# Joining the taps above and below in an HetConv stage: 64x32 tiles over a stacked copy of the image

## What is computed

```
x = x + _L1_conv_ref(_gn(x), L1_conv_W, L1_conv_b, 4)

_gn: 32 groups of 4 channels, mean and variance over (4, 32, 32), (v - m) / sqrt(s + 1e-5)
_L1_conv_ref:
    is3x3 = (i - n) % 4 == 0              # input channel i, output channel n
    Wm = W * where(is3x3, ones(3,3), centre only)
    y = conv 3x3, padding 1, of x with Wm
    return y + sum(b, axis=1)
```

## Time and profile before

| what | value |
|---|---|
| runs, median of three | 695.71 us (691.93 to 696.08) |
| profiled execution, device time | 695.91 us |
| its span in the trace | 694.0 us |
| mean granted TensorE clock | 0.957 |
| PE busy over the span | 586.4 us (84%) |
| DVE, ACT, POOL busy | 490.5, 489.1, 250.3 us |
| last stage, first to last `conv_done` | 461.18 to 685.71 us of the span |

### The profile page before, as it was taken

How to read it: one execution, slowest core, us unless ns; L and a number is a source line. 1 busy time by engine, 2 the same in 40 slices (tenths; PEclk the granted TensorE clock), 3 DMA queues, 4 the chain that set the end, 5 groups by cost and what they waited for, 6 DMA issues and landing times.

```text
span 694.0 us, 23636 instructions
## 1 busy us (share of the span) xinstructions
PE 586.4 (84%) x9897; PEld 416.7 (60%) x9897; DVE 490.5 (71%) x1172; ACT 489.1 (70%) x870; POOL 250.3 (36%) x253
## 2 busy tenths in 40 slices
PE   1899799899999999999999999386677876768882
PEld 1344344588888888888888887154454544444451
DVE  5788973599999999999999999864345454433220
ACT  2688688899999999999999998543335443333520
POOL 2478667445555555555555555300000000000000
PEclk9899899999999999999999999699999999998997
DMA  9989900022344444432224440013222333222343
GB/s 226 251 236 259 204 4 0 1 37 42 46 62 62 62 61 62 62 58 43 43 43 62 60 63 1 0 35 95 65 64 70 81 92 75 64 66 64 72 97 84
DMA packets 85002, 53.38 MB, mean 77 GB/s; under 512 B 71200, under 2 KB 72480, under 8 KB 84896
## 3 DMA queue, kind: packets, MB, share of 16 engines
q1 hardware_dynamic: 84224, 51.07, 36.9%
q10 hardware_dynamic: 672, 0.79, 0.5%
HBM read 35.07 MB, written 16.78 MB: 75 GB/s over the span
## 4 chain that ended last, share of the span: by engine, by line
PE 73%; issue 11%; DVE 8%; ACT 3%; SPq 1%; POOL 1%; DMA 1%; DVEq 0%; ACTq 0%; POOLq 0%
PE ps L1102 16%; PE ps L1181 15%; PE ps L1080 11%; PE ps L1107 8%; PE ps L1159 7%; PE ps L1084 5%; PE ps L1025 4%; PE ps L1026 3%; PE ps L1169 2%; DVE bn L416 2%; SPq L286 1%; DMA img<-in_x_dram 1%; POOL lo L755 1%; ACT xn L824 1%; ACT hi L834 1%
## 5 line engine op out<-in xcount | busy, mean ns | idle before, releaser
L1102 PE MATMUL ps<-z_hi,wg_hi 128*128 128x352 f32 (+13 forms) x384 | 134.2, 351 | 3.3 <-ACT z_hi L882 3.3
L774 POOL TENSOR_TENSOR fc<-gate,cell 128x352 f32<-128x352 f32 (+16 forms) x96 | 83.8, 873 | 144.1 <-ACT gate L898 144.1
L1102 PE MATMUL ps<-z_hi,wg_lo 128*128 128x352 f32 (+13 forms) x384 | 122.2, 319 | 0.0
L952 ACT ACTIVATE img<-ps,finish 128x512 f32<-128x512 f32 x32 | 23.1, 773 | 137.9 <-PE ps L1181 137.9
L1107 PE MATMUL ps<-z_lo,wg_hi 128*128 128x352 f32 (+13 forms) x384 | 107.5, 321 | 0.0
L898 ACT ACTIVATE gate<-ps,gate_bias 128x352 f32<-128x352 f32 (+16 forms) x192 | 104.1, 542 | 1.3 <-PE ps L1107 1.3
L683 DVE TENSOR_SCALAR img<-ps,finish 128x512 f32<-128x512 f32 x32 | 24.9, 805 | 110.8 <-PE ps L1181 110.8
L898 ACT ACTIVATE ps<-ps,gate_bias 128x352 f32<-128x352 f32 (+16 forms) x192 | 99.5, 518 | 0.0
L1181 PE MATMUL ps<-pad,wall_hi 32*32 32x512 f16 x3072 | 79.7, 408 | 15.9 <-issue 15.9
L784 POOL TENSOR_TENSOR img<-hT,xr 128x352 f32<-128x352 f32 (+1 forms) x96 | 88.6, 923 | 1.7 <-DVE hT L639 1.7
L755 POOL TENSOR_TENSOR lo<-xn,hi 128x1024 f16<-128x1024 f32 x32 | 68.0, 2131 | 32.4 <-ACT hi L834 31.8
(11 more groups left out here) (131 smaller groups left out, 1263.7 us busy)
## 6 DMA issues: line engine op xcount, KB each, us to landing
xr<-in_x_dram SPq DMA_DIRECT2D x64, 256.0 KB, 5.6
out_dram<-img SPq DMA_DIRECT2D x64, 256.0 KB
img<-in_x_dram SPq DMA_DIRECT2D x126, 128.0 KB, 3.6
raw_c<-in_L_conv_W_dram SPq DMA_DIRECT2D x4, 144.0 KB, 2.9
img<-in_x_dram ACTq DMA_DIRECT2D x2, 128.0 KB, 3.2
raw_g<-in_L_conv_w_ih_dram SPq DMA_DIRECT2D x1, 256.0 KB, 8.9
raw_i<-in_L_conv_w_i2s_dram ACTq DMA_DIRECT2D x1, 192.0 KB, 5.4
raw_s<-in_L_conv_w_s2s_dram ACTq DMA_DIRECT2D x1, 192.0 KB, 5.7
```

Of the source, the lines that this page charges most:

```text
L774: pool.tensor_tensor(fc[it % 2][:, 0:c1 - c0], gate[it % 2][0][:, 0:c1 - c0], cell[:, c0:c1], ALU.mult).then_inc(fc_done, 1)
L1102: pe.matmul(gbank(it, m)[:, 0:n], w[:, GATE_ORDER[m], :], z_hi[it % 2][:, 0:n], start=(w is wg_hi), stop=False)
```

## The change

The six taps above (d = 0) and below (d = 2) an image row no longer run as 32x32 tiles in groups 1 to 15. For every image from the third on, GpSimd copies the padded slot twice (`stack`, k = 0 and 1), and SyncE then overwrites, by four transfers from `pad`, the 32 partitions of the neighbouring class in each copy with the same class's image shifted by two rows. A 64-partition half of the stack so holds one class twice, as it stands and two rows further down, and one 64x32 tile multiplies it with the weights of both taps (`wk_hi`, `wk_lo`, placed once by sixteen small transfers). That is 3 terms x 3 columns x 2 x 8 = 144 matmuls; the side taps (`SIDES`) stay, 3 x 2 x 16 = 96. Group 0 keeps all of its 384.

The statistics are regrouped: of the upper image halves of eight images that VectorE measured during LSTM items 88 to 95, four are now measured during items 60, 68, 76 and 84, the other four images whole after the LSTM, between the first `lo` calls. The second chunk's `sum_means`, `sum_vars`, square root and `chain_rstd` come later in group 0.

```diff
+UPPER_AT = (60, 68, 76, 84)
+SIDES = [(1, 0), (1, 2)]
+TWO_ROWS = 2 * (W + 1)
...
+            stack = [[sb(f"stack{i}{k}", [P, PADT], F16, s2) for k in range(2)] for i in range(SLOTS)]
...
+            def place_blocks():
+                sp.wait_ge(split_done, 3 + 3)
+                for t, src in ((wk_hi, wall_hi), (wk_lo, wall_lo)):
+                    for q in range(Q):
...
+                        sp.dma_start(t[r, q % 2], src[r, 0, :, r]).then_inc(blocks_in, 16)
+                        sp.dma_start(t[other, q % 2], src[r, 2, :, r]).then_inc(blocks_in, 16)
+            def stack_below(b):
+                sp.wait_ge(stacked, 2 * (b - PAIR + 1))
+                for q in range(Q):
+                    sp.dma_start(stack[b % SLOTS][q % 2][32 * (q ^ 1):32 * (q ^ 1) + 32, 0:PADT - TWO_ROWS],
+                                 pad[b % SLOTS][32 * q:32 * q + 32, TWO_ROWS:PADT]).then_inc(below_in[b % SLOTS], 16)
...
+            stack_below(PAIR)
+            stack_below(PAIR + 1)
             for g in range(GROUPS):
                 sp.wait_ge(out_act, len(ACT_CLASSES) * (g + 1))
                 sp.wait_ge(out_dve, len(DVE_CLASSES) * (g + 1))
                 store_group(sp, g, range(Q))
+                for b in range(PAIR * (g + 2), min(PAIR * (g + 3), B)):
+                    stack_below(b)
...
-                if ITEMS - HELD <= it < ITEMS:
-                    if it == ITEMS - HELD:
-                        v.wait_ge(row_done, ROW_AHEAD + NB * H // 2)
-                    upper_stats(it - (ITEMS - HELD))
+                if it in UPPER_AT:
+                    v.wait_ge(row_done, ROW_AHEAD + NB * H // 2)
+                    upper_stats(UPPER_AT.index(it))
...
+                if g == 0:
+                    chain_var(FIRST_CHUNKS + 1)
+                    chain_rstd(FIRST_CHUNKS + 1, 1)
...
+            for b in range(PAIR, B):
+                pool.wait_ge(lo_done, b + 1)
+                if b >= PAIR + SLOTS:
+                    pool.wait_ge(conv_done, (b - SLOTS) // PAIR + 1)
+                for t in stack[b % SLOTS]:
+                    pool.tensor_copy(t[:].bitcast(F32), pad[b % SLOTS][:].bitcast(F32)).then_inc(stacked, 1)
...
+            def above_and_below(g):
+                for b in range(PAIR * g, PAIR * g + PAIR):
+                    pe.wait_ge(below_in[b % SLOTS], 16 * Q * ((b - PAIR) // SLOTS + 1))
+                for m, (w, part) in enumerate(TERMS):
+                    for e in range(3):
+                        for k in range(2):
+                            for c in range(Q):
+                                b, row = piece(g, c)
+                                at = LOW_AT * part + ROWS_AT + (row - 1) * PADW + e - 1
+                                for half in range(2):
+                                    r = slice(64 * half, 64 * half + 64)
+                                    pixels = stack[b % SLOTS][k][r, at:at + PIECE_ROWS * PADW]
+                                    ins = pe.matmul(rows(out_rows(g, 2 * half + k, c)), WK[w][r, k, e],
...
+                                                    stop=m == len(TERMS) - 1 and e == 2, tile_position=(64 * half, 32 * c),
...
             for g in range(1, GROUPS):
...
                 residual(g)
-                tiled(g, TERMS, True)
+                tiled(g, TERMS, SIDES, False)
+                above_and_below(g)
```

More of the change, by code:

```diff
@@ L133, in build_network @@
         wg_lo = sb("wg_lo", [P, GATES, P], F32R)
+        wk_hi = sb("wk_hi", [P, 2, 3, 32], F16)
+        wk_lo = sb("wk_lo", [P, 2, 3, 32], F16)
         class_of = sb("class_of", [P, Q], F32)
@@ L252, in build_network @@
         class_set = sem("class_set")
+        blocks_in = sem("blocks_in")
+        stacked = sem("stacked")
+        below_in = [sem(f"below_in{i}") for i in range(SLOTS)]
         ident_scaled = sem("ident_scaled")
@@ L370, in _ @@
                 load_x(b)
+            def place_blocks():
+                sp.wait_ge(split_done, 3 + 3)
+                for t, src in ((wk_hi, wall_hi), (wk_lo, wall_lo)):
+                    for q in range(Q):
+                        r = slice(32 * q, 32 * q + 32)
+                        other = slice(32 * (q ^ 1), 32 * (q ^ 1) + 32)
+                        sp.dma_start(t[r, q % 2], src[r, 0, :, r]).then_inc(blocks_in, 16)
[5 more added lines that the diff above has]
+                                 pad[b % SLOTS][32 * q:32 * q + 32, TWO_ROWS:PADT]).then_inc(below_in[b % SLOTS], 16)
             def load_rows(r):
@@ L380, in _ @@
             load_rows(1)
+            place_blocks()
             for r in range(2, H // 2):
@@ L416, in bn_stats @@
                     v.bn_stats(bn[:, j, s, :], src[:, 512 * s:512 * s + 512]).then_inc(bn_done, 1)
[L418 to L422, removed]
             def bn_aggr(g):
-                v.wait_ge(bn_done, bn_count(g))
+                v.wait_ge(bn_done, 2 * ENDS[g])
                 apart()
@@ L694, in _ @@
             v.wait_ge(row_done, ROW_AHEAD + ITEMS)
-            for b in range(CH, HELD):
-                lower_stats(b)
+            image_stats_again(CH)
+            image_stats_again(CH + 1)
+            lo(0)
+            image_stats_again(CH + 2)
+            lo(1)
+            image_stats_again(CH + 3)
             bn_aggr(FIRST_CHUNKS + 1)
-            lo(0)
-            lo(1)
+            lo(2)
             chain_mean(FIRST_CHUNKS + 1)
-            lo(2)
-            chain_var(FIRST_CHUNKS + 1)
-            chain_rstd(FIRST_CHUNKS + 1, 1)
+            lo(3)
             image_stats_again(HELD)
-            lo(3)
             image_stats_again(HELD + 1)
@@ L964, in _ @@
             norm(2)
-            square_root(FIRST_CHUNKS + 1)
             high(3)
@@ L973, in _ @@
                     finish_class(g, q)
+                if g == 0:
+                    square_root(FIRST_CHUNKS + 1)
                 if near < B:
@@ L1136, in _ @@
             WALL = {"hi": wall_hi, "lo": wall_lo}
+            WK = {"hi": wk_hi, "lo": wk_lo}
             def bank_free(g, q):
@@ L1171, in residual, with tiled @@
                                   tile_position=(32 * q, 32 * c), skip_group_check=True)
-            def tiled(g, terms, last):
+            def tiled(g, terms, taps, last):
                 for m, (w, part) in enumerate(terms):
-                    for d, e in TAPS:
+                    for d, e in taps:
                         for c in range(Q):
@@ L1181, in tiled @@
                                 ins = pe.matmul(rows(out_rows(g, q, c)), WALL[w][r, d, e, r], window(b, part, row, d, e)[r],
-                                                start=False, stop=last and m == len(terms) - 1 and (d, e) == TAPS[-1],
+                                                start=False, stop=last and m == len(terms) - 1 and (d, e) == taps[-1],
                                                 tile_position=(32 * q, 32 * c), skip_group_check=True)
@@ L1185, in tiled @@
                     ins.then_inc(conv_done, 1)
+            def above_and_below(g):
[11 more added lines that the diff above has]
+                                    ins = pe.matmul(rows(out_rows(g, 2 * half + k, c)), WK[w][r, k, e],
+                                                    pixels.rearrange("p (h w) -> p h w", w=PADW)[:, :, 0:W], start=False,
+                                                    stop=m == len(TERMS) - 1 and e == 2, tile_position=(64 * half, 32 * c),
+                                                    skip_group_check=True)
+                ins.then_inc(conv_done, 1)
             pe.wait_ge(split_done, 3 + 3)
             pe.wait_ge(ident_scaled, 1)
+            pe.wait_ge(blocks_in, 16 * 4 * Q)
             pe.wait_ge(gate_done, GATE_BANKS + GATES * ITEMS)
@@ L1194, in _ @@
             dense(0, TERMS[:2], True)
+            residual(0)
+            tiled(0, TERMS[:2], TAPS, False)
             sum_means(FIRST_CHUNKS + 1)
-            residual(0)
-            tiled(0, TERMS[:2], False)
             pe.wait_ge(lo_done, PAIR)
+            dense(0, TERMS[2:], False)
+            tiled(0, TERMS[2:], TAPS, True)
             sum_vars(FIRST_CHUNKS + 1)
-            dense(0, TERMS[2:], False)
-            tiled(0, TERMS[2:], True)
             for g in range(1, GROUPS):
```

## The result

The changed kernel took 642.92 us (median of four runs, 641.62 to 643.08), the kernel before 694.84 us, timed alongside (691.93 to 696.08). The ratio is 0.925, 95% interval 0.922 to 0.929. The change saves 52 us; the forecast was 653 us, so it is 10 us faster than forecast and inside the range of 628 to 677 us. The profiled execution has a span of 640.9 us.

A forecast was written before the change was run, and what follows sets the result against it. TensorE was taken to wait for instruction fetches: -4.21 us for fewer instructions and +1.4 for traffic make -2.8 us a group, -42 us over 15 groups; with statistics -0.7, 695.9 - 42.7 = 653 us, range 628 to 677.

The forecast's parts named there:

- What bounds the kernel: Last stage: TensorE waits for its own instructions, fetched in blocks of 256, one every 3.45 or 3.74 us.
- takes nothing off the bound: Rival: the waits come from something else at fixed places; period stays 14.97 us, time 695 us; chance 0.04.
- Fewer instructions, -4.21 us: Outer taps: 384 matmuls a group become 240, 1.125 instruction blocks fewer at 3.74 us each, -4.21 us a group.
- Array time: Six stacked taps: 18 rounds as before at 0.225 us, no change; work floor 9.4 us a group, counted at nothing.
- unhidden weight loads: Rival: loads of 64x32 tiles no longer run under matmuls; group 16.4 us if halves overlap, 717 us; chance 0.04.
- More traffic, +1.4 us: Stack transfers, 1.10 MB a group, slow instruction fetches as stores do: +1.4 us a group, ends 0 and +2.8.
- no disturbance by the copies: Rival: copies leave fetches alone; 10.8 us a group, 633 us, or 619 us at the work floor; chance 0.15.
- GpSimd, SyncE, placements: Copies 1.1 us each, 4.5 us a group; twelve SyncE transfers 7.3 us a group, fits; weight placements at LSTM's start cost nothing.
- The path of the stacks: Stacks land some 16 us after `conv_done`, needed at 17.2 us with period 12: hidden, thinly, by 1 us.
- Statistics, -0.7: LSTM: four fewer half-image statistics save 0.7 us in all; images 4 and 5 later counted nothing, else 1 to 2 us.

The follow-up runs named there:

- half_columns: The kernel before with each outer-tap matmul over half its image rows, same number of matmuls and weight loads: 703.24 us, ratio 1.012.
- split_sides: The changed kernel with each side-tap matmul of groups 1 to 15 cut in two of half the columns, 96 matmuls a group more: 688.17 us, 0.994.
- no_traffic: The changed kernel storing only the last group's output, with copies and stack transfers only for the first four images: 622.12 us, 0.895.
- interleaved: The changed kernel with dense and side taps taken in turn, term by term, same instructions: 641.70 us, 0.928.
- regroup_only: The kernel before with only the statistics regrouped, no stacks, copies, transfers or placements: 692.07 us, 0.998.
- taps_only: The changed kernel with the statistics grouped as before: 649.12 us, 0.935.
- store_between: The changed kernel with each group's store issued between the transfers into the two next stacks instead of ahead of both: 667.70 us, 0.959.

## Why the prediction was right, and where it was off

**What bounds the kernel: right.** With fewer pixels in the same instructions the blocks still come 3.45 us apart (`half_columns`); the same products in more instructions are slower, half of it by longer waits (`split_sides`). The rival "takes nothing off the bound" is refuted.

**Fewer instructions, -4.21 us: right in kind and in its price.** 3.74 us a block stood in the sum (its rows give 3.73); quiet fetches measure 3.71. The stage's packets fell from 55 to 38 (about 39 forecast). Of "issue" 2 to 3 us a group were forecast and 15.8 / 15 = 1.05 us are left. That crossing a block is mostly hidden, as the Trainium skill says (Runtime: NRT & Kernel Launch, Instruction fetch mechanics), describes the changed kernel better, with its 16 waits at 38 blocks, than the kernel before, with 33 at 55. By that rule alone, the prediction said, both kernels would stand at 9.3 us a group; neither does. But the price is only paid out down to the floor. Without any traffic the change moves the period from 13.51 to 10.11 us, 3.40 and not 4.21.

**Array time: the round right, the floor 0.7 us low.** Stacked rounds stand 0.225 us apart as forecast, and the rival of unhidden weight loads is refuted by that row: a round is shorter than its eight loads of 93 ns, even if the loads of the two halves ran side by side (0.37 us), so they go on while tiles of the same rows run. The rule of the Trainium skill (TensorE: Matmul & The Clock Gate, Part 3) that was weighed there, overlap only between different row groups, did not hold here, by 0.225 us a round. The floor was summed to 9.4 us and "counted at nothing"; `no_traffic` shows 10.11. Pieces of its chain:

```profile
508.03 4.13 PE ps L1239 x144
512.16 0.31 PE ps L1031 x2
```

Dense 2.78, residual 1.07, sides 1.54 (1.35 in the sum) and stacked 4.13 (4.05 in the sum) make 9.52. Two small statistics matmuls, some 0.32 us each (512.16 is one), stand on the chain in every second group; I had left them out. They bring 0.32 a group, 9.84 in all. What the last 0.27 us are is not shown piece by piece; short waits and the tails before them are part of it.

**More traffic, +1.4 us: the step that failed, by size.** The sum carried the store's 1.36 us over from the kernel before and added 1.4 us for the copies. Together 2.8 us a group; measured 11.42 - 10.11 = 1.31 us. The store's term was good for the kernel it was read from (1.27 to 1.46 measured there) and shrank to about 1.0 in the new one. The copies cost 0.2 to 0.4, and that is the larger part of the miss. Two things go into it. A copied megabyte is cheaper than a stored one even in the kernel before, where both meet bare fetches, ones that no work hides: 0.65 against 1.27 us by the medians. That was open by the rows, and I took the middle of nothing to 2.8 us where the truth lay between the low end and the middle. What makes it so, whether the memory that is written or the length of the rows, no run tells apart. The other is cover. Before, nearly every block that lay wholly in the taps ended in a wait, so a slower fetch was paid for. Now a block's end often falls behind dense or residual work, and a fetch that is slowed there costs nothing. I priced each megabyte as if all fetches were bare. The counts of waits fit this (31 before, 13 after in the taps), and `interleaved`, which moves only the cover at the same instructions and traffic, cut "issue" to 4.0 us.

The two errors partly cancel: +0.7 of floor, -1.5 of traffic, period 11.42 for 12.2, and 15 x 0.8 = 12 us of the stage. That the miss is not the 1.5 us a group of the traffic alone, 22 us, is luck. The rival "no disturbance by the copies" (633 us) lies as far from the measured 643 us as the forecast does, and in the price of the copies it was the nearer one; the floor, which it left out too, and the waits of the stacks kept the time above it.

**GpSimd, SyncE, placements: right.** A copy takes 1.11 us (1.1). Issues of 0.59 us; twelve a group fit. The placements cost the LSTM between 0.1 us (`regroup_only` to the change) and 0.7 us (before to `taps_only`) by the same profiles as below: nothing that a run could measure.

**The path of the stacks: right, and as thin as said.** SyncE's timeline behind the `conv_done` at 483.70:

```profile
490.99 3.14 SPq L396 DMA_DIRECT2D stack<-pad_first  x4
494.29 2.40 SPq L396 DMA_DIRECT2D stack<-pad  x4
```

The last issue ends at 496.69 and 2.8 us of landing make 15.8 us, where the prediction had 16. With a period of 11.4, not 12.2, the stack is wanted at 16.6. It was late once, 1.5 us: behind the `conv_done` at 597.67 a GpSimd pair took 3.18 us and a transfer 3.94 us to land, 17.4 us in all. Both `interleaved` and `store_between` used up the cover at once.

**Statistics, -0.7: the account was wrong, not the sign.** From the first to the last `z_lo` the LSTM takes 305.56 us before, 305.50 in `regroup_only`, 306.25 in `taps_only`, 305.65 in the change: 0.6 us saved in one pair, 0.1 in the other, one profile each, so between nothing and the forecast. The larger part lay where I counted "nothing; if it shows, 1 to 2 us", and with the other sign: images 4 and 5 becoming later does not show, image 3's stack becoming earlier does. Of the 6.2 us the two first periods alone make (14.0 + 12.7) - (11.6 + 10.9) = 4.2 us, the lower clock behind the late stack included.

## What to carry to other kernels

When an engine waits for nothing that the profile shows, count the instructions between two such waits: a constant count that also fits the packets of the instruction queue points to a fetch, and the cure is fewer instructions for the same work, not fewer pixels. Price a slower fetch only where it is bare, and sum the work floor to the last small matmul before leaving it out, since that is where the gain stops. A new producer path that fits by 1 us should be followed on the queue instruction by instruction: a store moved from the time in which its queue would only wait to a place between two stacks cost half of the gain here.

## What the runs showed of the hardware that I had not expected

- TensorE with half the pixels per outer-tap matmul was granted less clock, 0.75 over the stage where it had been 0.95, and ended later, 703 against 694 us.
- Transfers from SBUF to SBUF, with GpSimd's copies, cost the fetch-bound kernel before about half of what stores of the same size cost: 0.65 against 1.27 us a group by the medians, for 1.10 and 1.05 MB. In the changed kernel they left TensorE's waits for instructions as they were, 15.8 us with them and 15.4 without.
- Changing the order removed 11.8 us of "issue" and gained nothing measurable: 6.5 us came back as a busier TensorE and 2.2 us as waits for stacks and VectorE; the stage of the one profile is 2.3 us shorter, which the medians don't confirm.
- Halving a 32x32 matmul's columns from 512 to 256 took 128 of them from 2.04 to 1.45 us, not to half.
- SyncE's issue of such a transfer is 0.59 us mostly, and for some 1.5 us: two right behind a queued store in `store_between`.
